# A two-layer transformer kernel on one Trainium2 core: the last of 32 attention items and everything behind it taken out of the common loop and written as a sequence of its own

## The reference

```python
B, N, D, H = 8, 128, 128, 16            # HD = 8 channels per head in layer 1
h1 = modulate(ln(x), sh_msa, sc_msa)
x = x + attend(heads(h1 @ W_qkv)) @ W_proj + b_proj        # self-attention
h2 = modulate(ln(x), sh_x, sc_x)
x = x + attend(h2 @ W_q, ctx @ W_k, ctx @ W_v) @ W_out + b_out   # cross-attention
h3 = modulate(ln(x), sh_mlp, sc_mlp)
x = x + gelu(h3 @ W_fc1 + b_fc1) @ W_fc2 + b_fc2           # 128 -> 512 -> 128
```

## Time and profile before

| | |
|---|---|
| time before, median of 3 runs | 415.65 us (414.74 to 415.76) |
| the profiled execution, its own time | 415.27 us |
| its span (first to last instruction or transfer) | 412.9 us |
| outside the span | 2.37 us |
| mean granted TensorE clock | 0.992 of full speed |
| last matrix product ends | about 409.5 us |
| last residual on VectorE starts | 409.50 us |

### The profile page before, as it was taken

One profiled execution on the slowest core, in us unless ns is written; L12 is line 12 of the kernel. 1 busy time (PEld: TensorE's weight loads), 2 busy tenths in 40 slices (PEclk: granted clock), 3 DMA queues, 4 the chain that ended last, 5 costly groups with the idle time before them and its releaser, 6 DMA issues. The chain is left out here.

```text
span 412.9 us, 9912 instructions
## 1 busy us (share of the span) xinstructions
PE 380.3 (92%) x3599; PEld 286.9 (69%) x3599; DVE 321.2 (78%) x696; ACT 298.5 (72%) x1033; POOL 155.7 (38%) x147
## 2 busy tenths in 40 slices
PE   7789998999999999999999897989899999999866
PEld 3547676777777777777777576776677787777554
DVE  5699998998999888989898669583658888788440
ACT  2377786786877778878786875789578887887622
POOL 4565453523744334642427124420274811002020
PEclk9899999999999999999999999999899999999999
DMA  6325525233243121222222110000000000000000
GB/s 212 122 85 162 164 95 170 94 120 112 79 141 117 58 97 53 78 76 79 78 78 78 52 52 0 2 3 2 0 2 2 3 2 2 2 2 2 2 25 25
DMA packets 15954, 26.08 MB, mean 63 GB/s; under 512 B 3582, under 2 KB 5892, under 8 KB 15780
## 3 DMA queue, kind: packets, MB, share of 16 engines
q1 hardware_dynamic: 13572, 18.49, 12.6%
q0 software_dynamic: 1616, 5.97, 5.0%
q10 hardware_dynamic: 720, 1.00, 0.8%
HBM read 8.15 MB, written 0.52 MB: 21 GB/s over the span
## 5 line engine op out<-in xcount | busy, mean ns | idle before, releaser
L280 POOL TENSOR_TENSOR swp<-swp,small 128x512 f32<-128x512 f32 x64 | 81.9, 1293 | 123.1 <-PE bank L884 72.9
L406 ACT ACTIVATE prob<-bank,nmax 128x128 f32<-128x128 f32 x256 | 91.5, 391 | 5.0 <-DVE nmax L676 5.0
L501 ACT ACTIVATE raw<-bank,nmax 128x128 f32<-128x128 f32 x256 | 73.0, 393 | 13.1 <-DVE nmax L782 12.8
L406 ACT ACTIVATION_READ_ACCUMULATOR prob<-bank,nmax 128x1 f32 x256 | 59.3, 232 | 0.0
L782 DVE TENSOR_REDUCE nmax<-bank 128x4 f32<-128x512 f32 x64 | 41.2, 685 | 17.9 <-PE bank L884 17.8
L676 DVE TENSOR_REDUCE nmax<-bank 128x4 f32<-128x512 f32 x64 | 41.2, 685 | 17.1 <-PE bank L884 17.1
L683 DVE TENSOR_TENSOR prob<-prob,rz 128x512 f32<-128x512 f32 x64 | 50.3, 786 | 2.2
L884 PE MATMUL bank<-hT,wqkv 128*128 128x512 f32 x96 | 49.7, 603 | 1.1 <-ACT hT L389 1.1
L235 POOL TENSOR_TENSOR rstd<-vare,neg_half 128x4 f32<-128x4 f32 x12 | 12.4, 1033 | 96.3 <-DVE vare L611 96.1
L412 ACT ACTIVATE probT<-bank 128x512 f32<-128x512 f32 x32 | 19.1, 597 | 40.3 <-PE bank L970 40.3
L970 PEld LDWEIGHTS bank<-small,prob 128*128 128x128 f32 x256 | 28.6, 140 | 27.9 <-DVE prob L683 17.8
(11 more groups left out here) (111 smaller groups left out, 637.9 us busy)
## 6 DMA issues: line engine op xcount, KB each, us to landing
swp<-raw SPq DMA_DIRECT2D x128, 128.0 KB, 2.1
wqkv<-in_wqkv POOLq DMA_DIRECT2D x13, 256.0 KB, 3.3
wff<-in_wff POOLq DMA_DIRECT2D x1, 1024.0 KB, 6.0
wsq<-in_wsq POOLq DMA_DIRECT2D x1, 576.0 KB, 5.4
x<-in_x SPq DMA_DIRECT2D x2, 256.0 KB, 4.7
wqkv<-in_wqkv ACTq DMA_DIRECT2D x2, 256.0 KB, 5.8
wmod<-in_wmod POOLq DMA_DIRECT2D x1, 512.0 KB, 4.3
out_x<-x SPq DMA_DIRECT2D x2, 256.0 KB, 2.3
```

The costliest lines, as they stand in the source:

```text
L280: nc.gpsimd.tensor_tensor(four(swp[:, m % 2, f, :]), four(swp[:, m % 2, f, :]), sin[f], ALU.mult).then_inc(rope_sin[f], 1)
L406: last = nc.scalar.activation(prob[:, hh, bcols(u)], S[hh][:, bcols(u)], ACT.Exp, bias=nmax[:, s % 2, hh, u:u + 1], accum_out=zsum[:, s % ...
L501: last = nc.scalar.activation(prob1[:, s % 2, hh, bcols(u)], score_bank(s, hh)[:, bcols(u)], ACT.Exp, bias=nmax[:, s % 2, hh, u:u + 1])
```

## The change

Slots 31 to 38 are taken out of the loop. Each of TensorE, VectorE and ScalarE gets a function `last_items()` that lists its instructions in one explicit order. Besides the order, these things differ:

- Half 0's MLP is issued as four single `up` products placed between other steps, and its `down` is cut into products of c = 0 to 2 and of c = 3, with the transposes of half 1's last normalisation between them.
- `turn_back(6)` and `divide(6)` use bank W in place of Y. The modulation of half 0's last normalisation (`scale_shift(5, 0, Y)`), four instructions in slot 30, is cut into two and two, with the exponentials of item 31 between them.
- Bank O's last group is copied to oS in two parts: three items (384 columns), then the last (128 columns), with the loading of the gelu table between them. `prob_values1(31)` gets a wait for the first part, `turn_back(7)` one for the second ahead of its fourth transpose.
- The last copy of transposed probabilities (item 31, second head) goes from ScalarE to VectorE.
- Half 1's last normalisation is done by VectorE alone (`SPLIT_XN`), and the residual of half 0's MLP stands behind it and behind the modulation on VectorE.
- The last `down` is done by pairs of batches, batches 4 and 5 into bank W and 6 and 7 into Y, each with its own seed, its own half-sized addition and its own 128 KB store.

The diff, cut to its core:

```diff
-SPLIT_XN = [[1, 2, 3, 4, 5], [1, 2, 3, 4, 5]]
+SPLIT_XN = [[1, 2, 3, 4, 5], [1, 2, 3, 4]]
...
-    return s < RUN or s == ITEMS or s % RUN in (0, 2, 4)
+    return s < RUN or s % RUN in (0, 2, 4)
...
-            for half in range(2):
-                sp.wait_ge(x_sum[half], 6)
-                sp.dma_start(out[batches(half), :, :].rearrange("b t d -> t b d"), x[:, batches(half), :]).then_inc(
-                    stored, 16)
-            sp.wait_ge(stored, 32)
+            def store(first, end):
+                sp.dma_start(out[first:end, :, :].rearrange("b t d -> t b d"), x[:, first:end, :]).then_inc(stored, 16)
+
+            sp.wait_ge(x_sum[0], 6)
+            store(0, HALF)
+            for i in range(2):
+                sp.wait_ge(x_sum[1], 6 + i)
+                store(HALF + 2 * i, HALF + 2 * i + 2)
+            sp.wait_ge(stored, 48)
...
-            for half in range(2):
-                inv_std(half, 5)
-                normalise_first(half, 5)
+            inv_std(0, 5)
+            normalise_first(0, 5)
+            inv_std(1, 5)
...
-            def scale_shift(k, half, src):
+            def scale_shift(k, half, src, first=0, end=HALF):
 
                 act.wait_ge(ln_T[half], k + 1)
                 if src is O:
                     act.wait_ge(ln_h_dve[half], SPLIT_H[half].index(k) + 1)
                 act.wait_ge(mod_done, 1 if k < 2 else 2)
                 j = MODS[k]
-                for u in range(2 if k in SPLIT_H[half] else HALF):
+                for u in range(first, 2 if k in SPLIT_H[half] else end):
...
+            def evacuate_last_o1(first, end):
+
+                act.wait_ge(pv1, ITEMS - 4 + end)
+                act.wait_ge(back, 7)
+                nc.scalar.activation(oS[:, first * P:end * P], O[:, first * P:end * P], ACT.Copy).then_inc(os_out, 1)
...
+            def last_items():
+
+                scale_shift(5, 0, Y, 0, 2)
+                exp1(ITEMS - 1, 0)
+                exp1(ITEMS - 1, 1)
+                scale_shift(5, 0, Y, 2, HALF)
+                evacuate_last_o1(0, 3)
+                load_table(4, ACT.Gelu_apprx_tanh)
+                evacuate_last_o1(3, 4)
+                gelu(1, 0, 0, S[1])
+                gelu(1, 0, 1, W)
+                evacuate_attention(3)
+                gelu(1, 0, 2, X)
+                gelu(1, 0, 3, S[0])
+                scale_shift(5, 1, Y)
+                for c in range(FF):
+                    gelu(1, 1, c, (S[0], S[1], X, T[0])[c])
...
-                bank = Y if g else W
+                bank = W if g in (0, 6) else Y
...
+            def last_items():
+                row_max1(ITEMS - 1, 0)
+                row_max1(ITEMS - 1, 1)
+                for s in (ITEMS - 2, ITEMS - 1):
+                    copy_T1(s, 0)
+                    copy_T1(s, 1)
+                divide(6)
+                dve.wait_ge(o_norm, 7)
+                divide(7)
+                residual(4, 1, W, acc_done[1], 3)
+                ln_stats(5, 1)
+                ln_aggregate(5, 1)
+                ln_normalise(5, 1)
+                scale_shift_last(5, 1, W)
+                residual(5, 0, T[1], acc_done[0], 4)
+                for i in range(2):
+                    dve.wait_ge(acc_done[1], 4 + i)
+                    xs = x[:, HALF + 2 * i:HALF + 2 * i + 2, :]
+                    nc.vector.tensor_tensor(xs, xs, four((W, Y)[i][:, :])[:, 2 * i:2 * i + 2, :], ALU.add).then_inc(x_sum[1], 1)
...
+                if s == ITEMS - 1:
+                    pe.wait_ge(os_out, 8)
...
+                elif g == 6:
+                    pe.wait_ge(exps1[1], ITEMS - 1)
+                elif g == 7:
+                    wait_hT(5, 0)
...
+                    if (g, i) == (7, 3):
+                        pe.wait_ge(os_out, 9)
+                    last = nc.tensor.transpose((W if g in (0, 6) else Y)[:, bcols(i)], oS[:, bcols(i)], ident)
...
-                    pe.wait_ge(exps1[1], ITEMS)
+                    pe.wait_ge(gelu_done, 2 * FF + 2)
...
+            def last_items():
+
+                score1(31)
+                prob_values1(29)
+                transpose_probs1(30, 0)
+                transpose_probs1(30, 1)
+                turn_back(6)
+                transpose_probs1(31, 0)
+                prob_values1(30)
+                transpose_probs1(31, 1)
+                pe.wait_ge(exps1[0], ITEMS - 1)
+                up(1, 0, 0, S[1])
+                prob_values1(31)
+                turn_back(7)
+                pe.wait_ge(o_norm, 7)
+                up(1, 0, 1, W)
+                attention_T(3)
+                up(1, 0, 2, X)
+                project_attention(3)
+                up(1, 0, 3, S[0])
+                down(1, 0, T[1], end=3)
+                transpose_norm(5, 1, [Y, W])
+                down(1, 0, T[1], first=3)
+                pe.wait_ge(gelu_done, 3 * FF)
+                for c in range(FF):
+                    up(1, 1, c, (S[0], S[1], X, T[0])[c])
+                for i in range(2):
+                    seed("b_fc2", (W, Y)[i], 2 * i, 2 * i + 2)
                     for c in range(FF):
-                        up(1, 1, c, (S[0], S[1], X, T[0])[c])
-                    down(1, 1, W)
+                        pe.wait_ge(gelu_done, 3 * FF + c + 1)
+                        for u in (2 * i, 2 * i + 1):
+                            off = (3 * FF + c) * P
+                            last = mm((W, Y)[i][:, bcols(u)], gT[:, c, bcols(u)], wff[:, off:off + P], False, False)
+                    last.then_inc(acc_done[1], 1)
```

More of the change, by code:

```diff
@@ L390, in scale_shift @@
                                                 bias=mod[:, j + 1, b:b + 1], scale=mod[:, j, b:b + 1])
-                last.then_inc(ln_h[half], 1)
+                if end == HALF:
+                    last.then_inc(ln_h[half], 1)
             def evacuate_raw(m, f):
@@ L535, in l1_slot @@
                     evacuate_proj("cq", s // RUN - 1)
-                for run in range(3):
+                for run in range(2):
                     if s == RUN * run + 14:
-                        scale_shift(4 + run // 2, run % 2, Y)
+                        scale_shift(4, run, Y)
                 if s == 5:
@@ L549, in background1 @@
             def background1(s):
-                for run in range(RUNS):
-                    half, e = run % 2, RUN * run
-                    if s == e + 11:
+                for run in range(3):
+                    if s == RUN * run + 11:
                         evacuate_attention(run)
-                    if run == 3 and s == e + 14:
-                        scale_shift(5, 1, Y)
                 if s in (3, 6):
@@ L583, in _ @@
                 l0_slot(s)
-            for s in range(39):
+            for s in range(ITEMS - 1):
                 l1_slot(s)
+            last_items()
         @block.vector
@@ L839, in background1 @@
             def background1(s):
-                for run in range(RUNS):
-                    half, e = run % 2, RUN * run
+                for run in range(3):
+                    e = RUN * run
                     if run and s == e + 8:
@@ L876, in _ @@
                 l0_slot(s)
-            for s in range(39):
+            for s in range(ITEMS - 1):
                 l1_slot(s)
-            residual(5, 1, W, acc_done[1], 4)
+            last_items()
         @block.tensor
@@ L1218, in l1_slot @@
                     down(0, 1, Y, first=1)
-                for run in range(RUNS):
+                for run in range(3):
                     if s == RUN * run + 12:
                         project_attention(run)
-                    if s == RUN * run + 14 and run < 3:
+                    if s == RUN * run + 14:
                         transpose_norm(4 + run // 2, run % 2, [Y, Y])
```

43 lines of the change are left out of this document (6 added, 37 removed).

## The result

| | before | changed |
|---|---|---|
| median, first comparison | 415.19 us (414.30 to 415.76, 4 runs) | 410.04 us (409.60 to 411.72, 4 runs) |
| ratio | | 0.9891, 95% interval 0.9863 to 0.9919 |
| profiled execution: time, span, mean clock | 415.27, 412.9 us, 0.992 | 409.60, 407.5 us, 0.996 |

The change made the kernel faster, by about 1.1%, as forecast. As a ratio the forecast was 412.0 / 415.65 = 0.9912, which lies inside the measured interval; so these runs alone don't show that the change is worth more than was forecast.

A forecast was written before the change was run, and what follows sets the result against it. Bound by one line of dependence from the last attention item to the last store, with TensorE's written order across it. 3.1 - 0.1 + 0.27 + 0.3 = 3.6 us off took 415.65 to 412.0, range 411.0 to 413.6.

The forecast's parts named there:

- normalisation of four: Half 1's last normalisation, four batches on VectorE alone: 1.15 us, replacing GpSimd's pair of 1.58; gain so far 3.1.
- The sum: From the last attention items to the last store: 3.1 - 0.1 + 0.27 + 0.3 = 3.6 us gained.
- the pair order: Last MLP on TensorE: same 32 records but two short seeds for one, 0.1 us lost.
- the last store: End of the kernel: 128 KB store with its issue takes 2.4 us for 2.71, 0.3 gained.
- the wait for that addition: Around half 1's last normalisation: waiting for half 0's MLP addition was to be most of 0.9 us gained.
- The base: Whole kernel: median of 415.65 us for the kernel before, with runs spreading half a us to either side.
- The clock: Slower rival: TensorE's clock falls in the last MLP, 5.0 us more, 417.0; chance 0.04.
- Outside the span: Profiled execution: 2.37 us outside the span, added unchanged to the forecast span of 409.3 to give 411.7.
- The load that holds the last copy: Rival at the last 128-column copy: table load holds ScalarE beyond 1.48 us; 1.28 more would give 413.3; chance 0.09.
- The Trainium skill's drain of 1.38 us: At the gelu table load: 2.66 us in all per switch, making the sum 2.2 and the time 413.4.
- The single products in the way: Rival between `turn_back(7)` and the projection: one gelu and one `up` delay the steps by 1.5 us, 413.5; chance 0.13.
- The front gains nothing: Rival: `turn_back(7)` stays late, only normalisation and tail gain, 0.9 + 0.5, so 414.2 to 414.6; chance 0.07.

The follow-up runs named there:

- a4: Changed kernel with half 1's last normalisation shared again, GpSimd batches 0 and 1, VectorE 2 and 3: 411.22 us, ratio 0.9914.
- d3: Kernel before with 5 idle products ahead of `turn_back(0)` alone: 415.77 us, ratio 1.0014.
- d2: Kernel before with idle products in its tail alone, 6 ahead of the last transposes and 4 ahead of the last MLP: 414.15 us, ratio 0.9969.
- c1: Kernel before with idle products in three holes, 5 ahead of `turn_back(0)`, 6 ahead of the last transposes, 4 ahead of the last MLP: 413.69 us, ratio 0.9987.
- a2: Changed kernel, unchanged, measured and profiled once more: 410.41 us, ratio 0.9897.
- b1: Changed kernel with the gelu table loaded behind the last copy of bank O, not ahead of it: 410.26 us, ratio 0.9915.

## Why the prediction was right about the change and wrong about the time

Put 1.76 us on each time of the changed trace, and it stands on the clock of the old one, on which the prediction was written.

| step | forecast | measured |
|---|---|---|
| `prob_values1(31)` starts | 386.8 | 386.82 |
| copy of 128 columns, us | 0.35 (0.3 to 0.65) | 0.28 |
| `turn_back(7)` ends | 388.45 | 388.23 |
| projection's seed | 390.8 | 390.72 |
| projection's addition starts | 392.3 | 392.24 |
| normalisation of four, us | 1.15 (1.14 to 1.36) | 1.11 |
| last transposes | 396.95 | 396.76 |
| last MLP starts | 398.6 | 398.44 |
| last products end | 406.5 | 406.50 |
| last addition, us | 0.42 | 0.42 |
| span's end | 409.3 | 409.26 |

**The sum was right: 3.64 us against 3.6, and no step off by more than 0.22 us.** Some of that is errors that cancel. ScalarE got to the table load 0.2 earlier than forecast (load and primer end at 387.57, not 387.8), which brought `turn_back(7)` forward; the step from its end to the projection's seed took 2.49 in place of 2.35. The last MLP took 8.06 in place of 7.9, since the pair order costs 0.3 and not 0.1, and the last store gave 0.41 in place of 0.3. Parts were also undone on their own: single products 1.64 in the chain, shared normalisation 0.6, pairs 0.5, load position 0.4. Others were not, so that their shares are argued from the traces alone: `turn_back(6)` in the earlier hole, the last copy on VectorE, the modulation cut in two and the later addition of half 0's MLP. One share was put down wrongly: of the 0.9 gained around the normalisation, "most" was to be the wait for that addition, but a4, which keeps the addition out of the way, loses 0.6 by sharing the normalisation again.

**The base was wrong: this is the first step that failed.** The forecast took 3.65 off a median of three executions, 415.65, and allowed for "the runs' spread of half a us to either side", read from the same three numbers. Over 67 executions the kernel before has a median of 414.76 (mean 414.84), and single ones from 411.90 to 418.97. The early part alone moved the mark between 379.6 and 382.2 us over the profiles. A base of 415.65 in place of 414.84 put the forecast 0.81 us too high, whatever the change did.

**The clock had a sign that I didn't give it: the second step.** The prediction took the tail of 30.8 us as that of the kernel. It treated the clock as a risk of the new order only: "the old tail has gaps of 1.4 and 1.0 us around 400.05 and PEclk 1.00 behind them, and the new order fills these gaps". The row was true of that execution (the first gap is 1.51 in it, not 1.4). In 31 of 67 executions of before there was a second fall; the profiles of d3 and of the repeat of before show it behind just those gaps, and d2 and c1 show that it mostly goes when they are filled. The changed kernel had a second fall in 3 of 10. At equal clock, 0.996, the mean spans are 411.57 (36 executions) and 407.80 (7): 3.8 us apart, near the 3.64 of the tails. Over all executions they are 412.46 and 408.25: 4.21 apart. The 0.4 us between would be what the change saves in falls; the fall's price of 1.7 us by the difference in their shares (31 of 67, 3 of 10: 0.16) gives 0.3 of it. Ten executions are few: the shares alone don't show that the changed kernel falls less often.

**Outside the span: the third step.** The prediction added "the 2.37 outside it" unchanged. The kernel before spent 2.38 us there on average and the changed one 2.08, which gives 0.3 more. The experiments have a pattern here. By their medians all kernels with the old order lie between 2.30 and 2.40 us, and all with the new one between 2.05 and 2.16, but one: a4, the changed kernel with GpSimd's pair of the last normalisation put back, has 2.31 (six executions from 2.25 to 2.41, against 1.96 to 2.18 in the ten of the changed kernel). So this time goes with GpSimd's pair, and taking it out was worth some 0.9 us by the means of a4 and a2, 0.6 to 0.7 of it in the span and 0.2 outside. What takes the time outside the span no profile shows; that stays open.

Together: 412.0 forecast, less 0.81 for the base, 0.56 for the spans (4.21 less 3.65) and 0.30 outside them is 410.33, the mean of the ten executions. This only splits the difference into measured parts; it has to close. The median of the first comparison, 410.04, lies 0.29 lower still. The mean gain is 4.5 us, or 4.8 and 4.6 within the two comparisons. The 5.15 of the first comparison has about 0.6 of chance in it.

**The rivals.** The load that holds the last copy: out (b1, and the gapless rows 384.32 to 385.81). The Trainium skill's drain of 1.38 us for each switch (ScalarE: Activation LUTs, What ACT_TABLE_LOAD costs) was seen in none of these traces: 1.28 for the load, then the primer within 0.02 us. The single products in the way: out; the seed came 0.08 earlier than forecast. The front gains nothing: out; the projection's seed came 2.3 us earlier than before (390.72 against 392.98). The clock: real, and on the other side.

## What to carry to other kernels

Before you forecast from one profiled execution, ask whether it is a typical one: look in it for stretches of lowered TensorE clock and for holes that could cause one in the next execution, and take the base from as many runs as there are. Forecast the ratio or the gain as well as the time: here the gain was right within its interval and the time was not. Work placed into the waits of a dependent chain can be worth more than its own time, since it can also keep the clock up, as the single products did here; an undo of the order should be judged with the clock beside it. Measure a change from a mark behind which the kernels differ: the tail told effects of 0.4 us apart that the medians didn't (it repeated within 0.07 us in the four profiles whose tail is that of the changed kernel). But look at what lies outside the mark too: a4 lost some 0.2 us where no profile looks.

## What the runs showed of the hardware that I had not expected

- Holes of only 1.5 and 1.0 us, with one set of transposes between them, were followed by 1.2 GHz for about 3 us in two of three profiles and not in the third. By the mean clock, 40 of 79 executions had a second fall with the tail's holes open and 3 of 24 with them filled.
- The first fall, in the early part, lay behind the hole of 2.84 us (18 to 24 us) in 11 of 13 profiles without idle products there, at 11 to 15 us in one and at 27 to 31 us in one.
- Stores to memory landed in 2.3 us (256 KB), 2.1 (192 KB), 1.8 (128 KB) and 1.5 (64 KB).
- A copy of 128 columns from PSUM with no scale or bias took 0.28 us on ScalarE; those with both stand 0.38 us apart.
- Ten idle products in the hole of 2.84 us at the start removed the first fall in 3 of 10 executions and left one in 7, and the kernel didn't become faster.
- With GpSimd's two instructions of the last normalisation in the program, an execution spent some 0.2 us more outside the profiled span (2.31 against 2.05 to 2.16).
